# Windowed linear attention, one core: the full k, v convolution of the next strip ahead of q, and one joint wait ahead of the pooled out products

## The reference, cut to what matters

```python
qkv = jnp.einsum('nchw,oc->nohw', xw, qkv_w)      # xw: windows of 4 x 4
pooled = _avg_pool5(qkv)                          # 5 x 5 mean inside the window
msq = jnp.concatenate([qkv, pooled], axis=1)      # then by heads of 3 * 8 channels
q = jax.nn.relu(msq[..., :DIM])
k = jax.nn.relu(msq[..., DIM:2 * DIM])
v = msq[..., 2 * DIM:]                            # padded with a column of ones
kv = jnp.einsum('ngld,nglm->ngdm', k, v)
out = jnp.einsum('ngld,ngdm->nglm', q, kv)
out = out[..., :-1] / (out[..., -1:] + 1e-15)
...
y = jnp.einsum('nchw,oc->nohw', out, proj_w)      # then batch norm, and x + y
```

## Time and profile before

| what | value |
|---|---|
| median of 3 runs | 887.57 us (885.05 to 888.76) |
| the profiled execution's own time | 886.18 us |
| its span | 884.3 us |
| PE busy | 848.4 us (96%) |
| DVE, ACT, POOL busy | 699.9, 480.9, 658.9 us |
| chain that ended last | PE 94%, DVE 3% |
| mean granted TensorE clock | 0.998 |
| DMA queue | 59.52 MB, 20.0% of 16 engines' span |

### The profile page before, as it was taken

How to read it: one execution, slowest core, us unless ns; L and a number is a source line. 1 busy time by engine, 2 the same in 40 slices (tenths; PEclk the granted TensorE clock), 3 DMA queues, 4 the chain that set the end, 5 groups by cost and what they waited for, 6 DMA issues and landing times.

```text
span 884.3 us, 63772 instructions
## 1 busy us (share of the span) xinstructions
PE 848.4 (96%) x28322; PEld 693.0 (78%) x28322; DVE 699.9 (79%) x1252; ACT 480.9 (54%) x1349; POOL 658.9 (75%) x1624
## 2 busy tenths in 40 slices
PE   0789999999999999999999999999999999999997
PEld 0568888888888888888888888888888888888885
DVE  7758888887778888888777888888777777777776
ACT  0346565646465655555555556565656564646563
POOL 2558787878787878777878777787878787878781
PEclk9999999999999999999999999999999999999999
DMA  6122322111123323111113232211111111111111
GB/s 236 40 77 81 103 84 82 49 47 48 47 69 97 91 94 98 51 48 47 49 50 99 86 98 88 82 51 48 48 50 46 49 48 47 48 47 48 47 49 47
DMA packets 39081, 60.06 MB, mean 68 GB/s; under 512 B 8560, under 2 KB 33648, under 8 KB 39024
## 3 DMA queue, kind: packets, MB, share of 16 engines
q1 hardware_dynamic: 39024, 59.52, 20.0%
HBM read 19.38 MB, written 18.87 MB: 43 GB/s over the span
## 4 chain that ended last, share of the span: by engine, by line
PE 94%; DVE 3%; issue 1%; DMA 1%; SPq 0%; ACT 0%; DVEq 0%
PE ps L703 24%; PE ps L687 17%; PE ps L659 14%; PE ps L668 9%; PE ps L675 9%; PE ps L787 7%; PE ps L778 6%; PE ps L789 4%; PE ps L676 4%; DVE stats L453 1%; DMA x_all<-x 0%; DVE kvc_full L561 0%; DVE kvc_pool L561 0%; DMA vm_full<-v_full 0%; DVE kvc_full L509 0%
## 5 line engine op out<-in xcount | busy, mean ns | idle before, releaser
L366 ACT ACTIVATE vm_pool<-ps,cst 128x256 f32<-128x256 f32 x576 | 230.1, 480 | 0.0
L376 ACT ACTIVATE q_full<-ps 128x384 f32<-128x384 f32 x96 | 47.2, 491 | 281.0 <-PE ps L675 281.0
L561 DVE TENSOR_TENSOR kvc_full<-ps,cst 128x864 f32<-128x864 f32 x192 | 193.2, 1048 | 4.7 <-PE ps L687 4.7
L561 DVE TENSOR_TENSOR kvc_pool<-ps,cst 128x864 f32<-128x864 f32 x192 | 193.2, 1048 | 0.5 <-PE ps L687 0.5
L286 POOL TENSOR_TENSOR xd<-x_all,mean_t 128x384 f32<-128x384 f32 x95 | 78.6, 827 | 154.3 <-PE ps L676 137.8
L659 PE MATMUL ps<-wkv_sb,xn 128*128 128x256 f32 x576 | 141.4, 382 | 23.1 <-DVE xn L517 23.1
L264 POOL TENSOR_TENSOR x_all<-y_pool,x_all 128x96 f32<-128x96 f32 x380 | 148.9, 424 | 12.7 <-DVE x_all L567 7.2
L659 PEld LDWEIGHTS ps<-wkv_sb,xn 128*128 128x128 f32 x576 | 109.4, 191 | 33.2 <-issue 23.0
L703 PEld LDWEIGHTS ps<-kvc_full,q_full 64*32 64x32 f32 x9216 | 108.3, 105 | 26.0 <-issue 26.0
L292 POOL TENSOR_TENSOR xn<-xd,rstd_t 128x96 f32<-128x96 f32 x380 | 121.8, 367 | 8.1 <-DVE xn L517 0.7
L703 PE MATMUL ps<-kvc_full,q_full 64*32 64x72 f32 x9216 | 125.0, 230 | 0.6 <-DVE kvc_pool L561 0.6
(11 more groups left out here) (74 smaller groups left out, 1316.2 us busy)
## 6 DMA issues: line engine op xcount, KB each, us to landing
vm_full<-v_full SPq DMA_DIRECT2D x384, 54.0 KB, 1.9
out<-x_all SPq DMA_DIRECT2D x96, 192.0 KB, 1.9
x_all<-x SPq DMA_DIRECT2D x36, 384.0 KB, 3.4
x_all<-x SPq DMA_DIRECT2D x6, 768.0 KB, 7.9
cst<-consts SPq DMA_DIRECT2D x1, 170.0 KB, 11.0
wkv_sb<-wkv SPq DMA_DIRECT2D x1, 128.0 KB, 10.8
o_sb<-proj SPq DMA_DIRECT2D x1, 128.0 KB, 10.1
wq_sb<-wq SPq DMA_DIRECT2D x1, 64.0 KB, 10.6
```

The source lines that it names most:

```text
L366: last = act.activation(heads[:, e, :, :, 0:D], src, ACT.Copy, scale=col(C_VP + e))
L561: last = dve.tensor_tensor(kvc[:, g], src.to_broadcast(shape), own, ALU.mult)
```

## The change

PE: conv_q(s) moves from the end of step s - 1 into step s, behind conv_kv(s + 1) and ahead of the transposes. For the last strip it stands behind the loop. The wait for masked v (vm_f) of the next strip moves from ahead of the kv products to ahead of the pooled out products, where it joins the waits for residual and y; behind it stands one nop. ACT: copy_v(s + 1) goes ahead of the two relus of q. POOL: the subtraction of the mean goes ahead of the wait for q.

```diff
@@ POOL, normalise_and_pool
-                wait(pool, q_p, s - 1)
                 mean = mean_t[:, s:s + 1].to_broadcast([P, SP])
...
                 link(pool.tensor_tensor(xd[:], x_all[:, s * SP:(s + 1) * SP], mean, ALU.subtract), 1)
                 rows = xd[:].rearrange("p (r g e c) -> p r g e c", r=WS, e=EF, c=WS)
+
+                wait(pool, q_p, s - 1)
@@ ACT, step
+                if not is_first(s) and not is_last(s):
+                    copy_v(s + 1)
                 relu_q(s)
                 relu_q_pooled(s)
-                if not is_first(s) and not is_last(s):
-                    copy_v(s + 1)
@@ PE, kv_products
-                if isinstance(s, int) and s < 2:
+                if is_first(s):
                     pe.wait_ge(km_f, s + 1)
-                pe.wait_ge(vm_f, 16 * EF * (s + 1))
-                pe.nop(nofuse=True)
+                    pe.wait_ge(vm_f, 16 * EF * (s + 1))
+                    pe.nop(nofuse=True)
@@ PE, out_products_pooled
-                if is_first(s):
-
-                    pe.wait_ge(km_f, s + 2)
-                    pe.nop(nofuse=True)
-                elif is_last(s):
+                if is_last(s):
                     pe.wait_ge(kvc_p, s + 1)
-                    pe.nop(nofuse=True)
                 else:
-
-                    pe.wait_ge(added_f, s)
-                    pe.wait_ge(y_copied, s)
-                    pe.nop(nofuse=True)
+                    pe.wait_ge(vm_f, 16 * EF * (s + 2))
+                    if is_first(s):
+                        pe.wait_ge(km_f, s + 2)
+                    else:
+
+                        pe.wait_ge(added_f, s)
+                        pe.wait_ge(y_copied, s)
+                pe.nop(nofuse=True)
@@ PE, step
                 if not is_first(s):
                     conv_kv(s + 1, p)
+                conv_q(s, 1 - p)
+                if not is_first(s):
                     transposes(s - 1)
...
                 kv_products(s + 1)
                 kv_products_pooled(s + 1)
-                conv_q(s + 1, p)
@@ PE, around the loop
-            conv_q(0, 0)
             step(0, 1)
             with pe.Fori(1, NS - 1, 2) as s:
                 step(s, 0)
                 step(s + 1, 1)
+            conv_q(NS - 1, 1)
```

## The result

The changed kernel takes **915.29 us** (median of 4 runs, 914.19 to 915.55), the kernel before 886.31 in the runs beside it (884.42 to 888.76): 1.0323 times as long, interval 1.0292 to 1.0353. The forecast was 928, its range 900 to 938.

What follows compares the result with a forecast made beforehand. PE was taken as the bound, with no other engine making it wait in the loop. 886.2 + 24.4 (q's wait) + 9.4 (second wait) + 8.1 (jump) = 928.1, so 928 us; range 900 to 938.

Steps and rivals of the forecast that it cites:

- 17.5 us for waits and jump: On PE: 9.4 us for a second wait ahead of the pooled out products, 8.1 us for the loop's jump.
- q's wait: At conv_kv_pooled: PE waits for ACT's relu of pooled q, 0.26 us in each of 94 strips, 24.4 us.
- in time after all: Rival at conv_kv_pooled: q's relus come early enough, 24.4 us goes and 9.4 us is gained: 877 us; chance 0.03.
- The register operation moved (+0.10 and -0.10): From ahead of the kv products to ahead of the pooled out products: 0.10 us removed, 0.10 us added, cancelling.
- the second wait (+0.10): Ahead of the pooled out products: a new second wait instruction costs 0.10 us in each of 94 strips, 9.4 us.
- queue hides the sequencer: Rival: PE's register operations, waits and jump pass while matmuls are queued; only q's wait costs: 901 us; chance 0.12.
- The place ahead of the kv products (-0.10): With nothing left ahead of the kv products, pooled out to kv products fall from 1.09 to 0.99 us.
- The jump (8.1 us): At the loop's jump: conv_kv's wait and weight loads can't be issued ahead, 0.18 us for each of 46 jumps.
- lower bound ("the rows of the jump move ahead with it"): At the loop's jump: 0 us, because the sequencer's rows of the jump come earlier too.
- The premise that no other engine makes PE wait: In the loop, a strip costs what PE's own order costs, 8.75 us; a step moved elsewhere gains nothing.

Runs made afterwards that it cites:

- experiment 3: The changed kernel with pooled q's matmul and its relu put ahead of the full ones: 892.05 us.
- experiment 1: The changed kernel with only the move of q (ACT's and POOL's part included), the waits put back where they were before: 901.75 us.
- experiment 4: The changed kernel with one more wait instruction, two semaphores reached long before (kvc_p, kvc_f), ahead of the pooled out products: 923.41 us.
- experiment 5: The kernel before, with the register value for vm_f computed early, behind conv_kv and the transposes among full-size matmuls: 885.36 us.
- experiments 5 and 6: Besides experiment 5: half of DVE's pooled own heads left out, in the kernel before (884.20 us) and in experiment 5's kernel (878.22 us).
- 7b: The kernel of experiment 1, with v's four transfers held back until the strip's conv_kv_pooled is done: 978.0 us.

## Why the prediction was right, and where its sizes were off

The time alone does not settle it: 915.3 lies 12.7 us below the forecast and 14.3 above the rival's 901. The stages do. Of the forecast's terms the wait for q holds; of the 17.5 us for waits and jump the loop shows some 3. That the time is no further off is in part luck, since 2.8 us that were not forecast came on top.

*q's wait (24.4 us): right, in place and size.* Forecast 0.26 us a strip, 0.26 in the strip above and 0.243 when it is taken out (experiment 3); also that conv_kv_pooled is 1.10 long and that all of it lies on PE's path. The rival "in time after all" fell with it.

*The register operation moved (+0.10 and -0.10) and the second wait (+0.10): the prices held, the base didn't.* The sequencer's entries ahead of the pooled out products, in the changed kernel, one narrow window each (starts 409.47, 409.57, 409.68):

```profile
L750 PEldq ALU_OP  x1: 36/36/36, 409.5 to 409.5; - x1
...
L756 PEldq EVENT_SEMAPHORE  x1: 51/51/51, 409.6 to 409.6; - x1
...
L757 PEldq EVENT_SEMAPHORE  x1: 51/51/51, 409.7 to 409.7; - x1
```

0.10 us apart, and the weight load at 409.76. The place takes 1.22 where the kernel with one wait and no register operation takes 1.00 (experiment 1), and a further wait adds 0.104 (experiment 4): about 0.10 for each entry beyond the first wait, as forecast. But the forecast added 0.20 to the 1.10 of before, taking that for the bare stage. It held a pause of 0.10 beside v's transfers, which went away as v moved. So the place grew by 0.11 to 0.13 and not by 0.20: 94 x 0.09, some 8 us too much. The rival "queue hides the sequencer" (901) falls for the small products: their further entries show in full. Among full-size matmuls, where experiment 5 put the register operation, nothing shows, as the rival had it. The kernel that comes out near its time, experiment 1, has no second wait to hide. The Trainium skill (TensorE: Matmul & The Clock Gate, the table that opens the page) gives TensorE a queue of 64 that pulls weight loads ahead of matmuls; that these entries are hidden as well is what the rival added to it, and the trace denies that part alone.

*The place ahead of the kv products (-0.10): -0.08 measured.* The first kv product comes 0.92 us behind the first pooled out product (410.71 and 409.79), where 0.99 was forecast: with nothing between them in the list, the weight loads of the kv products begin before the last pooled out products. The next full-size stage comes only 0.08 earlier.

*The jump (8.1 us): wrong, it costs nothing.* The step took the branch to be tied to the last kv products and kept their distance. The branch and the next turn's first wait in the changed kernel (starts 411.90 and 412.26):

```profile
L823 PEldq COMPARE_BRANCH  x1: 208/208/208, 411.9 to 411.9; - x1
...
L194 PEldq EVENT_SEMAPHORE  x1: 51/51/51, 412.3 to 412.3; - x1
```

They are 0.36 us apart, as in the earlier trace rows, but the branch starts 0.55 ahead of the first full-size matmul (412.45), and in the kernel before 0.26 ahead of conv_q's (415.65 and 415.91). By the list, what it had stood behind is the issuing of conv_q's own instructions, which were the last of a turn and have gone from there. The prediction named this as its lower bound ("the rows of the jump move ahead with it") and chose the middle; the strips with a jump are no longer than those without. The branch's record is 208 ns here too, not the 108 ns of the Trainium skill (Advanced Engine Details and Errata, Control Flow Timing), but nothing hung on it.

*Not foreseen: 2.8 us at the start.* In the first three strips, the first passage of each piece of the code, PE stands on "issue" for 2.38, 1.66 and 2.66 us, where before it stands 1.87, 1.50 and 2.19: 1.1 of the 2.8. The rest is TensorE's clock. Behind the first of these idle times the granted clock is 0.50 in the changed kernel, the 1.2 GHz level. Experiment 4 has the same list up to there and the same idle time, and keeps 1.00. The first pooled kv products of the changed kernel, with the window 42 to 45 us (us, PE busy, granted clock, DMA share, GB/s), and of experiment 4:

```profile
41.39 1.54 PE L686 MATMUL ps<-vm_pool,k_pool 64*32 64x216 f32 x31 [2.38 <-issue]
...
42.00:45.00 3.00, 3.00 (x28) 0.50 0.02 5
...
41.39 0.96 PE L686 MATMUL ps<-vm_pool,k_pool 64*32 64x216 f32 x31 [2.37 <-issue]
...
42.00:45.00 3.00, 3.00 (x28) 1.00 0.03 5
```

The next full out products start at 49.10 in the changed kernel and at 47.46 in experiment 4: 1.64 us. The kernel before keeps 1.00 here too; a later stretch at 0.50, near 62 to 69 us, all three have. So 1.6 of the 29.2 us between the two profiled executions come from how the clock fell in this one, not from the new order in each strip.

*The premise that no other engine makes PE wait* was good enough for this forecast, but it held by little: experiments 5 and 6 show DVE's way to project to be about as long as the strip of the kernel before.

Together: 886.2 + 22.8 + 94 x (0.11 - 0.08) + 2.8 = 914.6, and 915.4 was measured.

## What to carry to other kernels

Where small matmuls bound a stage, count TensorE's register operations and all waits beyond the first as work, satisfied or not (about 0.10 us each here), and put the register operations among full-size matmuls, where experiment 5's passed unseen. When a producer moves, follow its consumer's relu to the wait that needs it and turn the order inside the stage first: here two swapped matmuls gave back 22.8 us. Before adding to a stage's measured length, ask what that length already holds, by a kernel that lacks the suspected part.

## What was not expected of the hardware

A further wait instruction whose semaphores were reached long before costs 0.104 us between streams of small matmuls (experiment 4). A transfer of some 0.3 us beside such a stream can hold its weight loads up (0.09 us in the full out products of the kernel before, 0.29 by two transfers in the pooled ones of 7b), though not always. And the clock: with v held back in the kernel before, PE stood idle for 2.85 us in each strip. Busy time by stretch there (window: us, PE, PEld, DVE, ACT, POOL busy, granted clock, DMA share, GB/s):

```profile
405.10:407.95 2.85, 0.01 (x1) 0.00 (x0) 1.22 (x4) 0.00 (x0) 1.65 (x5) 1.00 0.24 82
407.95:409.40 1.45, 1.41 (x48) 1.44 (x56) 0.00 (x0) 0.00 (x0) 0.00 (x0) 0.50 0.87 178
409.40:411.06 1.66, 1.66 (x47) 0.77 (x28) 1.28 (x2) 0.00 (x0) 0.00 (x0) 0.50 0.52 197
411.06:412.30 1.24, 1.24 (x11) 0.97 (x5) 1.24 (x2) 0.16 (x1) 0.00 (x0) 0.88 0.00 0
```

Behind that idle time the granted clock is 0.50, the 1.2 GHz level, for both kv products, and back at 2.4 GHz while q's convolution runs. The kv products take 411.06 - 407.95 = 3.11 us there, 1.65 in the earlier trace rows: a wait of 2.85 us cost 1.46 more. It does not always: in 16 of the strips 6 to 89 the clock stays at 1.00, and they last 11.65 us, where the others last 13.3 on average. That is part of why this kernel's time was missed so far.
